# Two transformer layers with expert routing: x kept in memory, gated rows added into it by the scatters

## The reference, cut to what matters

```
x = x + tanh(g_xattn[0]) * attention0(x_normed, ctx)
x = x + tanh(g_ffn[0])   * sum over the 2 chosen experts of  gate * expert(x_normed)
x = x + tanh(g_xattn[1]) * attention1(x_normed, ctx, mask, causal)
x = x + tanh(g_ffn[1])   * sum over the 2 chosen experts of  gate * expert(x_normed)
```

## Time and profile before

| what | us |
|---|---|
| median of 3 runs | 1868.79 (1862.5 to 1886.18) |
| the profiled execution | 1870.4 |
| its span, first to last instruction | 1868.4 |
| attention of layer 0 with its start and end | about 0 to 500 |
| experts of layer 0 | about 500 to 980 |
| attention of layer 1 | about 980 to 1460 |
| experts of layer 1 | about 1460 to 1829 |
| loads, adds and stores at the end | 1829 to 1868 |

### The profile page before, as it was taken

How to read it: one execution, slowest core, us unless ns; L and a number is a source line. 1 busy time by engine, 2 the same in 40 slices (tenths; PEclk the granted TensorE clock), 3 DMA queues, 4 the chain that set the end, 5 groups by cost and what they waited for, 6 DMA issues and landing times.

```text
span 1868.4 us, 36398 instructions
## 1 busy us (share of the span) xinstructions
PE 1658.6 (89%) x12444; PEld 1568.0 (84%) x12444; DVE 1220.9 (65%) x2877; ACT 1198.4 (64%) x2795; POOL 790.8 (42%) x877
## 2 busy tenths in 40 slices
PE   3999999998399999999985999999994699999990
PEld 2898899897399999999983888888893699999990
DVE  2566666655477777777756667777755566666655
ACT  1676666664288888888853666666671477777760
POOL 2123333324356666666652113333322366666660
PEclk8999989987599999999997999999995799999995
DMA  2112221212477777778743222222220677777758
GB/s 93 45 47 64 68 54 44 57 40 88 121 228 226 234 234 230 230 223 234 228 152 95 64 63 81 79 79 82 57 75 32 184 236 231 235 233 227 231 181 278
DMA packets 209512, 265.58 MB, mean 142 GB/s; under 512 B 28224, under 2 KB 155460, under 8 KB 209200
## 3 DMA queue, kind: packets, MB, share of 16 engines
q1 hardware_dynamic: 189840, 222.36, 41.3%
q0 software_dynamic: 13632, 35.13, 5.2%
q10 hardware_dynamic: 5856, 5.77, 1.0%
HBM read 202.89 MB, written 45.69 MB: 133 GB/s over the span
## 4 chain that ended last, share of the span: by engine, by line
PE 78%; DVE 9%; issue 4%; DMA 4%; POOL 3%; ACT 2%; SPq 1%; DVEq 0%; POOLq 0%; ACTq 0%
PE ps L373 20%; PE ps L375 19%; PE ps L374 19%; PE ps L490 10%; PE ps L393 5%; POOL xs_scr L1156 2%; PE ps L500 2%; PE ps L409 1%; DMA U<-ys_scr 1%; DVE mx L914 1%; PE ps L416 1%; PE ps L471 1%; DVE X L935 1%; DVE X L1355 1%; DMA xs_scr<-U,PI 1%
## 5 line engine op out<-in xcount | busy, mean ns | idle before, releaser
L1060 POOL TENSOR_TENSOR KXR<-U,KXR 128x1024 fp32r<-128x1024 f32 (+1 forms) x156 | 334.5, 2144 | 307.8 <-ACT KXR L650 307.0
L373 PE MATMUL ps<-QR,KXR 128*128 128x256 f32 x1248 | 355.5, 285 | 8.5 <-DVE QR L1064 8.5
L374 PE MATMUL ps<-QR,KXR 128*128 128x256 f32 x1248 | 354.8, 284 | 0.0
L375 PE MATMUL ps<-QR,KXR 128*128 128x256 f32 x1248 | 354.5, 284 | 0.0
L650 ACT ACTIVATE KXR<-U 128x1024 fp32r<-128x1024 f32 (+1 forms) x312 | 287.8, 949 | 78.0 <-PE ps L375 63.5
L561 ACT ACTIVATE U<-ps,mx 128x128 f32<-128x128 f32 x1024 | 292.5, 382 | 6.3 <-DVE mx L914 5.7
L490 PEld LDWEIGHTS ps<-VA,U 128*128 128x128 f32 x2048 | 269.6, 200 | 9.5
L914 DVE TENSOR_REDUCE mx<-ps 128x4 f32<-128x512 f32 x256 | 175.5, 686 | 132.1 <-PE ps L409 67.3
L490 PE MATMUL ps<-VA,U 128*128 128x17 f32 x2048 | 259.8, 260 | 0.0
L373 PEld LDWEIGHTS ps<-QR,KXR 128*128 128x128 f32 x1248 | 238.8, 191 | 9.8 <-DVE QR L1064 9.8
L374 PEld LDWEIGHTS ps<-QR,KXR 128*128 128x128 f32 x1248 | 239.0, 191 | 0.0
(11 more groups left out here) (191 smaller groups left out, 4024.1 us busy)
## 6 DMA issues: line engine op xcount, KB each, us to landing
U<-in_wpack SPq DMA_DIRECT2D x234, 512.0 KB, 4.1
U<-xs_scr SPq DMA_DIRECT2D x78, 257.0 KB
U<-in_wpack SPq DMA_DIRECT2D x78, 256.0 KB, 3.5
KXR<-U SPq DMA_DIRECT2D x512, 32.0 KB
U<-in_ctx_t SPq DMA_DIRECT2D x16, 512.0 KB, 3.9
U<-ys_scr SPq DMA_DIRECT2D x32, 256.0 KB, 2.8
U<-ys_scr SPq DMA_DIRECT2D x16, 512.0 KB, 10.8
XR<-in_L_ffn_b SPq DMA_DIRECT2D x39, 128.0 KB, 3.9
```

The lines of the kernel that those rows point to most:

```text
L373: e.matmul(o, wh, xh, start=first, stop=False)
L374: e.matmul(o, wh, xl, start=False, stop=False)
L375: return e.matmul(o, wl, xh, start=False, stop=done)
L1060: e.tensor_tensor(w_cols(L, WL, n), w_raw(L, n), hi, ALU.subtract).then_inc(*l_w[n](L, i))
```

## The change

x is also kept in DRAM. Each group of X is stored after its attention update, in layer 0 to a new tensor `x1_scr`, in layer 1 into `out` (8 DMAs of 512 KB per layer, at step 16g + 25, from SP). The gate times tanh(g_ffn) is written into a second extra column of the rows (ROW = 258), so it travels with the row to its expert. The result rows are multiplied by it: in layer 0 by POOL (two new TENSOR_SCALAR per tile in `pool_y`), in layer 1 by ACT as the scale of the copy that was there. The indirect DMAs then add these rows into the stored x (`compute_op=ALU.add`, bounds 4096 rows), and both choices of a token go to the same row. A repeated tile would add twice, so its token numbers are raised beyond the bound (`su`). Layer 1 loads X again from `x1_scr` (8 DMAs of 512 KB, group 0 right behind `experts_out`, the others at step 16g - 24); its adds on DVE are gone, and so are the loads, adds and stores at the end.

```
-ROW = D + 1
+ROW = D + 2
-            c[:, C_TOK + k * B + b] = k * T + b * S + p
+            c[:, C_TOK + k * B + b] = b * S + p
-        ys_d = [nc.dram_tensor(n, (2 * T, D), F32, kind="Internal").ap() for n in ("ys_scr", "ys1_scr")]
+        sum_d = [nc.dram_tensor("x1_scr", (T, D), F32, kind="Internal").ap(), A["out"].rearrange("b s d -> (b s) d")]
...
+            w.wait_ge(*v_xi[1, i])
             for a in range(2):
-                e.activation(yo[:, i % 2, a], YB[a][:, 0:D], ACT.Copy).then_inc(*a_y(1, i, a))
+                e.activation(yo[:, i % 2, a], YB[a][:, 0:D], ACT.Copy, scale=xg[:, i % 4, a:a + 1]).then_inc(*a_y(1, i, a))
...
-            e.tensor_scalar(GT[:, L, :, p.bs], GA[:, L, :, p.bs], th[:, 2 + L:3 + L], None, ALU.mult).then_inc(*v_ga(*k))
+            e.tensor_scalar(xr(p.g)[:, :, p.js, D + 1:D + 2].rearrange("p z g o -> p z (g o)"), GA[:, L, :, p.bs], th[:, 2 + L:3 + L], None, ALU.mult).then_inc(*v_ga(*k))
...
-                if L == 1:
-                    for j in range(G):
-                        if (g := grp(s, -3 + j)) is not None:
-                            b = g * G + j
-                            w.wait_ge(*d_yl[b % 2][b])
-                            e.scalar_tensor_tensor(X[:, b], YL[:, b % 2, 0], GT[:, 0, 0, b:b + 1], X[:, b], ALU.mult, ALU.add).then_inc(*v_c.up())
-                            w.wait_ge(*v_c.now)
-                            e.scalar_tensor_tensor(X[:, b], YL[:, b % 2, 1], GT[:, 0, 1, b:b + 1], X[:, b], ALU.mult, ALU.add).then_inc(*v_yl(b))
...
-                        w.wait_ge(*(v_yl[b] if L else d_x[g][g]))
+                        w.wait_ge(*(d_xl if L else d_x)[g][g])
...
+            e.tensor_scalar(su[:, :], ti, tl[:, 2, E - 1:E], float(4 * T), ALU.is_gt, ALU.mult).then_inc(*v_c.up())
...
             if i >= 4:
                 w.wait_ge(*d_fy[i % 2][L, i - 4, 1])
-            e.tensor_copy(xi[:, i % 4], xt[:, i % 2, :, D]).then_inc(*v_xi(L, i))
+                w.wait_ge(*(a_y if L else p_y)[L, i - 4, 1])
+            e.tensor_copy(xg[:, i % 4], xt[:, i % 2, :, D + 1]).then_inc(*v_c.up())
+            if i < E:
+                ins = e.tensor_copy(xi[:, i % 4], xt[:, i % 2, :, D])
+            else:
+                w.wait_ge(*v_c.now)
+                ins = e.tensor_scalar(xi[:, i % 4], xt[:, i % 2, :, D], su[:, i - E:i - E + 1], None, ALU.add)
+            ins.then_inc(*v_xi(L, i))
...
         def pool_y(e, w, L, i):
             r = i % 2
             w.wait_ge(*v_xi[L, i])
+            if L == 0:
+                for a in range(2):
+                    w.wait_ge(*v_y[0, i, a])
+                    e.tensor_scalar(yo[:, r, a], yo[:, r, a], xg[:, i % 4, a:a + 1], None, ALU.mult).then_inc(*p_y(0, i, a))
             if i:
                 w.wait_ge(*d_fy[1 - r][L, i - 1, 1])
+            else:
+                w.wait_ge(*d_xs[L, NG - 1])
             for a in range(2):
-                w.wait_ge(*m_y[L][L, i, a])
-                e.indirect_dma_start(ys_d[L], bass.IndirectOffsetOnAxis(ap=xi[:, i % 4, a:a + 1], axis=0), yo[:, r, a, :], None,
-                                     bounds_check=2 * T - 1, oob_is_err=False).then_inc(*d_fy[r](L, i, a))
+                w.wait_ge(*(a_y if L else p_y)[L, i, a])
+                e.indirect_dma_start(sum_d[L], bass.IndirectOffsetOnAxis(ap=xi[:, i % 4, a:a + 1], axis=0), yo[:, r, a, :], None,
+                                     bounds_check=T - 1, oob_is_err=False, compute_op=ALU.add).then_inc(*d_fy[r](L, i, a))
...
-                if L == 0 and (g := grp(s, -8)) is not None and g:
-                    sp_load_x(e, g)
-                if L == 1:
-                    for j in range(G):
-                        if (g := grp(s, -5 + j)) is not None:
...
+                if (g := grp(s, -8)) is not None and g:
+                    sp_load_x(e, L, g)
+                if (g := grp(s, 41)) is not None:
+                    w.wait_ge(*v_xup[L, (g + 1) * G - 1])
+                    e.dma_start(sview[L][:, g * G:(g + 1) * G, :], X[:, g * G:(g + 1) * G, :]).then_inc(*d_xs(L, g))
...
             experts_out(w, 1)
-            ysv = ys_d[1].rearrange("(k b p) d -> p k b d", k=2, p=128)
...
+            w.wait_ge(*d_xs[1, NG - 1])
```

## The result

The changed kernel takes 1898.71 us as the median of 4 runs (1896.14 to 1909.33), beside 1867.57 of 4 runs of the kernel before: 1.6% longer, ratio 1.0164 with a 95% interval of 1.01 to 1.0227. The profiled execution has a span of 1895.5 us, against 1868.4.

The account below looks back on a forecast made before the run. PE was taken to bound both expert stages, with no matmul in the last 38.9 us. Terms -39.6 - 11 - 1.3 + 9 = -42.9 from 1868.4 gave 1825.5, 1826 after adjusting to the runs' median; range 1816 to 1836.

Parts of the forecast that it names:

- POOL's spare time, layer 0: Layer 0's experts: POOL's low part ends 2.47 us before PE's `pe_up`, enough to cover 2.3 us added per tile.
- The multiplications: POOL, layer 0's experts: two new multiplications at about 0.42 us each, 1.0 us per tile with the hand-over (0.8 to 1.7).
- The scatter's issue: POOL, experts: issuing an adding scatter takes +0.5 us in layer 1, +0.65 in layer 0; bounds nothing to +1.0 and +1.3.
- first rival: Experts: POOL becomes the bound if issuing an adding scatter takes twice as long; 1889 us, slower than before; chance 0.17.
- Layer 1's experts: POOL's two longer scatter issues add 1.0 us per tile against 1.39 to spare, so they cost nothing.
- The landing: Experts: the adding scatter's landing grows from 4.8 and 3.9 us under load but stays hidden unless it nearly doubles.
- second rival: Experts: the landing doubles to 7.8 us in layer 1 and becomes the bound, PE waits 15 us: 1841; chance 0.10.
- The end: Program end: loads, adds and stores behind the last scatter's landing go, 39.6 us less.
- The two ends of the experts: Last two tiles' scatters of each layer follow one another: +5.0 us in layer 0, +4.0 in layer 1, together 9.
- The adds in layer 1's attention: Removing DVE's 64 adds ends PE's 2.2 us wait in five groups: 11 us less, bounds 4 to 13.5.
- third rival: Layer 1's attention keeps its period because PE then waits for ACT or the projections' low parts: 1837 us; chance 0.10.
- The start of layer 1: Without DVE's first adds, DVE takes the first K projection's low part sooner: 1.3 us less.

Follow-up runs that it names:

- e9: Kernel before, plus one POOL multiplication of 128x256 by 1.0 ahead of each tile's scatter in layer 0: 1887.08 us, beside 1862.70 for the kernel before.
- e10: e1's kernel with DVE's `XS` and the small instructions behind it moved ahead of the last low part of the hidden rows in layer 0: 1844.65 us.
- e1: Changed kernel without POOL's multiplications by the gate in layer 0 (rows added ungated): 1867.05 us.
- e4: Changed kernel with POOL's low part of weight quarter 0 ahead of the scatters instead of behind them, all work done: 1846.45 us.
- e6: Changed kernel without POOL's multiplications in layer 0 and with plain scatters in place of adding ones in both layers: 1826.79 us.
- e8: Kernel before without the loads of expert rows and the 64 DVE adds in layer 1's attention: 1867.78 us, beside 1873.73 for the kernel before.
- e5: Changed kernel with DVE's two small instructions of a tile (`xg`, `xi`) behind its two low parts of the weights instead of ahead: 1920.28 us.
- e3: Changed kernel with the old conversion of token numbers for every tile, without the offset `su` that drops repeated tiles: 1893.31 us.

## Why the prediction was wrong, step by step

It forecast 1826 us and faster; the change is slower by 31 us. Two steps failed, both in layer 0's experts: the cover, "2.47 us to spare. [...] Nothing else stands between POOL and PE there", and a term of the sum, "Two and the hand-over to the DMA: 1.0 us". Something does stand there, and the two take 2.6.

- **POOL's spare time, layer 0.** The cover was counted from the end of POOL's low part to PE's first matmul. Between them stand DVE's held low part and `XS`: 0.70 us were free, as e9 shows, and e10 against e1. Less 0.70, the prediction's own sum of 2.3 leaves 1.6 a tile, some 60 us, and a slower kernel.
- **In the changed kernel POOL is later still.** PE waits there for POOL's low part itself in 31 of 36 tiles and for `XS` in four, so the whole 2.47 is used up, and e4 and e6, which take the work from ahead of that low part, return the tile to 11.9.
- **The multiplications were mis-sized.** 0.42 each was scaled from a pass of 128x512 in 0.63; they take 1.22 as a mean, 1.64 in e4 where they run beside DVE's low parts. The two and their hand-over (7.3 us in 36 waits) are 2.6 us, not 1.0. The two-input row of the same size, 0.73, was nearer and still too low.
- **The scatter's issue** lay within its bounds: 1.66 for 1.30 as a mean, +0.73 a tile in layer 0, where 1.3 was taken; 1.57 for 0.98 in layer 1, +1.17, where 1.0 was taken. The rule "slower from 1.85 in layer 1" of the first rival was not reached.
- **The sum for layer 0** is then 2.6 + 0.7 = 3.3 a tile. Against 2.47 this is 0.9 a tile, 33 us, which would still have left the change a little faster or the same. Measured is 1.56, 59 us. What is missing is POOL's wait for DVE's result rows, a term that the prediction put at nothing. As means over 33 tiles, counted from one first matmul of `pe_up` to the next, POOL's low part of quarter 3 begins 0.7 us earlier than before and takes 0.3 longer, the wait behind it is 1.0 longer, and with the 3.3 the low part of quarter 0 ends 4.0 later (at 13.35 for 9.36). Less 2.47 this is 1.5. The rows come late because the two low parts ahead of them on DVE are held (2.06 us each as a mean instead of 1.21). No run takes away this wait alone, so its share is read from the trace, not shown by an experiment.
- **Layer 1's experts.** 1.17 and 0.2 for the longer low part of quarter 3 (1.46 instead of 1.28) fill the 1.39 entirely: "fit, barely" was 0.23 us a tile too good, 8.9 us.
- **The landing** was right: 4.7 and 5.3 us under load, hidden. The second rival did not happen. By the estimate from the Trainium skill's "Collectives: The Full Stack", section "The bandwidth ceiling: the fold count and why AG ≠ RS ≠ AR", it would double; the trace has 4.8 to 4.7 in layer 0 and 3.9 to 5.3 in layer 1, and 2.7 for 2.3 where the scatter has the queues to itself.
- **The end** was right: behind the last `XS` 33.6 us less, where 39.6 less 4.0 for the last scatters, 35.6, was expected. The last scatter starts at 1889.00 and lands about 2.7 later, and the span ends some 3.8 us behind that.
- **The two ends of the experts.** Layer 0's last scatter lands 33.6 us after the last `XS` instead of 26.4, +7.3 where 5 was taken; in layer 1 it is +2, where 4 was taken.
- **The adds in layer 1's attention** brought nothing, not 11 us: the number of the third rival, given one chance in ten, but not its mechanism. PE's waits did fall, by 0.5 us at `RK` and 0.5 at `U`, and a group at the upper level of the clock by 1.2 us instead of the 2.2 forecast, because 1.2 of the 1.7 at `RK` was not the adds'. Then the granted clock was only 0.94 in two of the groups (0.90 to 0.97 in other kernels), and the sum was as before. The prediction had no term for the clock there.
- **The start of layer 1** took 3.5 us less (first `RK` 141.4 instead of 144.9 after the last landing), where 1.3 was taken, but the granted clock there was 0.93 instead of 0.91; without the adds it was 144.7 at 0.87 in e8 and up to 149.3 at 0.84 in e5. So what the removed adds give there is not shown.
- **"Free"**: the stores, the reloads and the wider rows cost nothing that a run shows. The reloads are half as many bytes as the loads that went, not as many: 8 DMAs of 512 KB for 32 of 256. DVE's small instructions were priced at 0.3 us a tile if their cover went. They are held for up to 6 us; to take one away or to move both gives back little in layer 0 (0.16 us a tile in e3, nothing in e5), and about 4 of layer 1's 8.9 us (e3, e5).

The first rival, POOL as the bound, was the right one by its place, but it was priced by the issue of the scatter alone and made to decide at 1.85 us. (The lower end of the forecast's own range, 1816, is 1815.4 by its sum; nothing hangs on it.)

## What to carry to other kernels

The spare time of an engine is not the gap to the bottleneck's next instruction: read what the engines between them do in that gap, above all instructions that are longer there than elsewhere, because their end moves with it. Work added to POOL ahead of a low part also moves the end of the DVE instructions that this low part holds, and what they delay can come back to POOL as a wait. Put the pass that others wait for first, and let ACT or a DVE instruction that reads PSUM take the arithmetic. Where a wait of PE gets shorter, read the granted clock of the same stretch beside it: in layer 1's attention 1.2 us a group were gained at the upper level and lost again at the lower.

## What the runs showed of the hardware

- POOL's low parts (TENSOR_TENSOR, both inputs in SBUF) hold DVE instructions whose operands all lie in SBUF, to the end of the pass and whatever their size: `xi` of 128x2 0.23 us alone and 3.70 beside one pass (the longest seen 6.02, beside two in a row), the hidden low part 0.69 and 4.06. `XS`, which reads PSUM, kept its 0.67 to 0.69 in every kernel. POOL's multiplication (TENSOR_SCALAR of 128x256, its rows and gates in SBUF) does not hold them so: 63 hidden low parts that ran beside it alone in the changed kernel took 0.67 to 0.96 us, 0.69 as the median. Who began first also counts: in e9 layer 0, 22 low parts of DVE that began ahead of POOL's kept their 1.21 us, and POOL's took up to 3.44 instead of 2.42, while 11 that began behind took 3.4. The Trainium skill's "SBUF — State Buffer", section "Who interferes with whom", says that a DVE instruction with two SBUF inputs contends with a GpSimd instruction that reads SBUF, and that copies and TENSOR_SCALAR can be blocked as a whole; the rows beside POOL's low parts agree, those beside its multiplication show next to nothing of it.
- An indirect DMA that adds took POOL 1.55 to 1.59 us to issue for 128 rows (medians of layer 1 and layer 0, at most 2.09), where the plain one took 0.98 to 1.30 as a mean.
- A TENSOR_SCALAR of 128x256 on POOL took 1.01 (a constant) and 1.22 us (a column) as a mean beside a working DVE.
- In layer 1's attention the granted clock was 1.00 with the adds (PE busy 48.6 of 51.3 us a group) and fell to 0.50 for 6.8 us in a group of e8, without them (48.35 of 50.1 in the group ahead of it).
